# Two state rows of 64 channels in one step of a Mamba scan, with silu and softplus as single ScalarE functions

## What is computed

```python
xz = u @ W_in;  xr, z = split(xz)              # 192 channels each
x = silu(causal_conv4(xr) + conv_b)
dt, Bm, Cm = split(x @ W_x)                    # 6, 16, 16 columns
delta = softplus(dt @ W_dt + b_dt)
A = -exp(A_log)                                # 192 x 16
h_t = exp(delta_t * A) * h_(t-1) + (delta_t * x_t) * B_t     # per channel and state n
y_t = sum over n of h_t * C_t
out = ((y + x * D) * silu(z)) @ W_out
```

## Time and profile before

| | |
|---|---|
| median of 3 runs | 2221.36 us (2218.45 to 2224.84) |
| the profiled execution | 2221.17 us, span 2219.4 us |
| busy, share of the span | PE 82%, DVE 88%, ACT 51%, POOL 88% |
| granted TensorE clock, mean | 0.94 |
| DMA | 398 MB, mean 179 GB/s |

### The profile page before, as it was taken

The page is one execution under the profiler, slowest core; times in us unless marked ns, Lnnn a source line. Parts: engine busy times, 40 slices in busy tenths (PEclk is TensorE's granted clock), DMA queues, the critical chain, the costliest instruction groups (busy, mean ns, idle before and its releaser), DMA issues. The chain is left out here.

```text
span 2219.4 us, 16413 instructions
## 1 busy us (share of the span) xinstructions
PE 1823.8 (82%) x4490; PEld 698.3 (31%) x4490; DVE 1958.8 (88%) x1276; ACT 1136.3 (51%) x1316; POOL 1957.2 (88%) x856
## 2 busy tenths in 40 slices
PE   5597889798798799789879779879878888876777
PEld 2232233233233333233333223323323333222322
DVE  2898898778998998998999898999889899899995
ACT  3657464645745644644655544644575564453331
POOL 0897988797998997998999899799899989899995
PEclk9798899899999899999999999999999999999898
DMA  3465556436556656664655665565655665566673
GB/s 83 170 206 147 173 176 176 139 130 222 157 189 213 175 170 204 175 197 172 206 156 197 217 176 199 190 162 190 207 155 173 202 191 185 192 205 184 219 218 81
DMA packets 119592, 398.24 MB, mean 179 GB/s; under 512 B 17788, under 2 KB 22156, under 8 KB 119500
## 3 DMA queue, kind: packets, MB, share of 16 engines
q1 hardware_dynamic: 119500, 397.20, 57.7%
HBM read 386.70 MB, written 6.29 MB: 177 GB/s over the span
## 5 line engine op out<-in xcount | busy, mean ns | idle before, releaser
L898 POOL TENSOR_TENSOR ring<-ring,c_ring 128x1024 f32<-128x1024 f32 x576 | 1348.4, 2367 | 113.7 <-DVE ring L835 110.6
L495 PE MATMUL y_ps<-ring,wp 128*128 128x512 f32 x2304 | 1183.8, 627 | 53.0 <-DVE yv_rows L815 28.2
L835 DVE TENSOR_TENSOR_SCAN ring<-a_ring,b_ps 128x1024 f32<-128x1024 f32 x424 | 968.2, 2284 | 28.5 <-ACT a_ring L616 0.3
L495 PEld LDWEIGHTS y_ps<-ring,wp 128*128 128x128 f32 x2304 | 449.9, 199 | 525.0 <-issue 409.6
L801 DVE TENSOR_TENSOR b_ps<-u_ab,b_ps 128x1024 f32<-128x1024 f32 x256 | 310.2, 1212 | 95.6 <-PE b_ps L487 69.2
L616 ACT ACTIVATE a_ring<-delta_ab,neg_a 128x1024 f32<-128x1024 f32 x256 | 290.6, 1142 | 199.2 <-DVE ring L835 194.0
L835 DVE TENSOR_TENSOR_SCAN ring<-b_ps,b_ring 128x1024 f32<-128x1024 f32 x152 | 344.6, 2273 | 27.7 <-ACT b_ps L616 12.3
L892 POOL TENSOR_TENSOR b_ring<-u_ab,b_ring 128x1024 f32<-128x1024 f32 x128 | 306.6, 2396 | 59.2 <-DMA b_ring<-b_rows 59.1
L616 ACT ACTIVATE a_ring<-delta_m,neg_a 128x1024 f32<-128x1024 f32 x168 | 192.3, 1145 | 238.8 <-DVE ring L835 238.7
L487 PE MATMUL b_ps<-b_in,sel 96*128 96x512 bf16 x512 | 164.2, 404 | 102.1 <-DVE ring L835 101.4
L801 DVE TENSOR_TENSOR b_ps<-u_m,b_ps 128x1024 f32<-128x1024 f32 x168 | 203.0, 1209 | 19.6 <-PE b_ps L487 19.6
(11 more groups left out here) (91 smaller groups left out, 1262.0 us busy)
## 6 DMA issues: line engine op xcount, KB each, us to landing
c_ring<-c_rows SPq DMA_DIRECT2D x384, 512.0 KB, 4.8
c_ring<-c_rows SPq DMA_DIRECT2D x384, 256.0 KB, 4.1
b_ring<-b_rows SPq DMA_DIRECT2D x128, 512.0 KB, 4.8
b_ring<-b_rows SPq DMA_DIRECT2D x48, 256.0 KB, 5.2
out<-io SPq DMA_DIRECT2D x16, 192.0 KB, 2.4
io<-x SPq DMA_DIRECT2D x6, 384.0 KB, 4.9
b_in<-parts SPq DMA_DIRECT2D x36, 64.0 KB, 2.0
dt_in<-parts SPq DMA_DIRECT2D x72, 24.0 KB
```

Source lines behind the costliest of these rows:

```text
L495: nc.tensor.matmul(half(y_ps[:, :], j), ident, half(ring[:, g % RING, :], j), start=(n == 0), stop=(n == NS - 1)).then_inc(g_summed, 1)
L835: nc.vector.tensor_tensor_scan(out=h, data0=a, data1=b, initial=0.0, op0=ALU.mult, op1=ALU.add).then_inc(h_ready, 1)
L898: nc.gpsimd.tensor_tensor(r, r, c_ring[:, g % C_RING, :], ALU.mult).then_inc(g_ready, 1)
```

## The change

A step now treats 64 channels and two states: partitions 0 to 63 hold the channels with state 2m, partitions 64 to 127 the same channels with state 2m+1. Two steps g and g+1 (sub 0 and 1) cover the tile's 128 channels for the two states. So an item still has 48 steps. What follows from it:

- delta and u are made once a tile (`delta_in`, `u_in`) and copied by eight DMAs of 64 x 1024 into doubled forms (`delta`, `u_two`); all users of them wait for these (`wait_two`).
- The two steps of a pair share a row pair of C in tiles 0 and 1: `c_ring` has three slots for four, and a slot serves two steps there and one in tile 2. Each load of C or B is two DMAs to 64 partitions.
- The sum uses a matrix of two stacked identities of 64 (`stack`). A job sums one column half of two steps: sub 0 into partitions 0 to 63 of `y_ps`, sub 1 into 64 to 127. SUM_LAG is 3.
- Silu and softplus are one ScalarE function each, without halved weights. Silus, gates and dts are put in twos; table loads stand between them and the exps.
- `x_out` and `parts3` hold one half instead of two, and "bc_in" comes twice.
- BY_POOL has 156 steps, and the slot tables of PREP, POST and the first items are new.

```diff
-BY_POOL = {ROWS: (2, 8, 13, 17, 19, 23, 26, 30, 31, 37, 47),
...
+BY_POOL = {ROWS: (5, 8, 14, 18, 20, 23, 25, 28, 31, 37, 41, 43, 47), FWD: (5, 10, 13, 15, 19, 20, 23, 25, 35, 41, 42),
+           BWD: (0, 6, 8, 13, 15, 19, 21, 23, 25, 31, 33, 39, 40, 45, 47)}
...
-PE_ORDER = ("ahead", "sum_0", "jobs", "sum_1")
+PE_ORDER = ("ahead", "sum", "jobs")
...
+PREP = dict(xr=(0, 2, 4.5, 6.5, 8.5, 10.5), silu=(4, 4, 8.5, 8.5, 12.5, 12.5), skip=(14, 16, 16), dbl=(14.5, 19),
+            dt=(25, 25, 34, 34, 52.2, 52.2), u=(26, 35, 54), two=(32, 48, 64), z=(20, 22, 24, 24, 27, 27))
...
+                elif name == "two":
+
+                    q = phase_of(kind, pair, i)
+                    wait(sp, h_ready, NS * (q - 1))
+                    sp.wait_ge(K["set_ready"][kind], 3 * pair + nth(i))
+                    for src, dst in ((delta_in, delta), (u_in, u_two)):
+                        for sub in range(2):
+                            for e in range(2):
+                                sp.dma_start(dst[e * DM:(e + 1) * DM, q % 2, sub, :],
+                                             src[sub * DM:(sub + 1) * DM, :]).then_inc(two_loaded[q % 2], 16)
...
+            def sum_half(pair_of, j):
+
+                n = 2 * pair_of % NS
+                pe.wait_ge(g_ready, 2 * pair_of + 2)
                 if n == 0:
-                    wait(pe, y_taken, 2 * (g // NS - 1) + j + 1)
-                nc.tensor.matmul(half(y_ps[:, :], j), ident, half(ring[:, g % RING, :], j),
-                                 start=(n == 0), stop=(n == NS - 1)).then_inc(g_summed, 1)
...
+                for sub in range(2):
+                    last = nc.tensor.matmul(half(y_ps[sub * DM:(sub + 1) * DM, :], j), stack,
+                                            half(ring[:, (2 * pair_of + sub) % RING, :], j),
+                                            start=(n == 0), stop=(n == NS - 2))
+                last.then_inc(g_summed, 1)
...
-                    nc.scalar.activation(half(xs[:, k, :], j), src, ACT.Identity, bias=bias)
-                    nc.scalar.activation(src, src, ACT.Tanh, bias=bias).then_inc(th_ready, 1)
...
+                    table("silu_and_others")
+                    empty(u, nc.scalar.activation(half(xs[:, k, :], j), src, ACT.Silu, bias=sm[:, m_of(k), 4:5]))
...
+                    table("softplus")
+                    empty(unit, nc.scalar.activation(half(delta_in[:, :], j), src, ACT.Softplus, bias=sm[:, m_of(k), 5:6]))
...
-                wait(dve, g_summed, 2 * (g - RING + 1))
+                wait(dve, g_summed, 2 * ((g - RING) // 2 + 1))
```

More of the change, by code:

```diff
@@ L33 @@
 RING = 6
-C_RING = 4
+C_RING = 3
 C_LEAD = 3
@@ L87, in fills_prep @@
         out.append((at["xr"][u] + 1, "xr", u))
-        out.append((at["xr"][u] + 2, "silu", u))
+        out.append((at["silu"][u], "silu", u))
     for k in range(TILES):
@@ L97, in fills_prep @@
     for k in range(TILES):
-        out.append((at["exp"][k], "dt_exp", k))
-        out.append((at["ln"][k], "dt_ln", k))
         out.append((at["u"][k], "u", k))
+        out.append((at["two"][k], "two", k))
     if kind != BWD:
@@ L197, in plan @@
         parts.append(item(FWD, p - 1, *fills))
-        parts.append(item(BWD, p - 1, fills_prep(ROWS, p + 1) if p + 1 < PAIRS else fills_prep(FWD, p)))
-    parts.append(item(FWD, PAIRS - 1, fills_post(BWD, PAIRS - 2), fills_prep(BWD, PAIRS - 1)))
-    parts.append(item(BWD, PAIRS - 1))
+        prep = fills_prep(ROWS, p + 1) if p + 1 < PAIRS else fills_prep(FWD, p)
+        parts.append(item(BWD, p - 1, late, own(prep)))
+        late = spill(prep)
+    prep = fills_prep(BWD, PAIRS - 1)
+    parts.append(item(FWD, PAIRS - 1, late, fills_post(BWD, PAIRS - 2), own(prep)))
+    parts.append(item(BWD, PAIRS - 1, spill(prep)))
     parts.append(alone(fills_post(BWD, PAIRS - 1)))
-    step = unit = use = 0
+    step = unit = 0
     for part in parts:
@@ L209, in plan @@
                 takes = name in BANKED
-                tanh = name in ("xr", "z")
-                slot[n] = (name, kind, pair, i, unit if takes else None, use if tanh else None)
+                slot[n] = (name, kind, pair, i, unit if takes else None)
                 unit += takes
-                use += tanh
     return parts
@@ new lines, in job @@
+                    sp.wait_ge(K["c_cut"][kind], 2 * pair + i + 1)
+                    wait(sp, g_ready, STEPS * (n - 1))
+                    sp.dma_start(half(b_rows[slot].rearrange("b n t -> (b n) t"), i), x_out[0:B_ROWS, :]).then_inc(c_kept, 16)
+                    sp.dma_start(half(c_rows[slot].rearrange("b n t -> (b n) t"), i), x_out[C_AT:X_ROWS, :]).then_inc(c_kept, 16)
+                    if n:
+                        landed(sp, "dt", ITEMS[n - 1]["kind"], ITEMS[n - 1]["pair"], 4, 5)
@@ new lines, in job @@
+                    landed(sp, "dbl", kind, pair, i)
+                    for g in range(3):
+                        sp.dma_start(half(b_in[B_ROWS * g:B_ROWS * (g + 1), slot, :], i),
+                                     parts3[0:B_ROWS, g, :]).then_inc(K["bc_loaded"][kind], 16)
+                    for q, (g, _) in enumerate(DT_TERMS):
+                        sp.dma_start(half(dt_in[2 * RANK * q:2 * RANK * (q + 1), :], i),
+                                     parts3[B_ROWS:SPLIT_ROWS, g, :]).then_inc(K["dt_loaded"][kind], 16)
+                elif name == "two":
[7 more added lines that the diff above has]
+                                             src[sub * DM:(sub + 1) * DM, :]).then_inc(two_loaded[q % 2], 16)
```

423 lines of the change are left out of this document (187 added, 236 removed).

## The result

The changed kernel took 2302.16 us (median of 4 runs, 2297.41 to 2314.84), the kernel before 2222.16 us beside it: a ratio of 1.037, 95% interval 1.0326 to 1.0414. The change made it slower by 80 us. The forecast was 2126 us, with 0.11 for slower.

The account below looks back on a forecast made before the run. VectorE and GpSimd, 88% busy each and joined by a ring of six buffers, were taken to bound the kernel together, with waits between. Terms -81 -15 -45 +10 +21 +9 -7 +13 = -95 from 2221.2 gave 2126 us; range 2065 to 2190.

Parts of the forecast that it names:

- Engines' work, -81: VectorE loses 87 us of work and GpSimd 75 net; both engines need it, so the mean, -81 us, was counted.
- the tanh waits (-15): VectorE's waits for ScalarE's tanh, 21 us, are removed; some will be found again before the scan: -15 us (0 to -21).
- ScalarE's batches, +21: Batch at slot 4, with its table loads, delays B's spread 1.9 us on 11 items: +21 us (0 to +50); other batches nothing.
- Sums, -45: Sums by 64 columns run side by side on TensorE, halving VectorE's 88.8 us wait for B's spread: -45 us (0 to -89).
- TensorE gives nothing: Rival, chance 0.17: TensorE's sum halves don't overlap or its clock falls, so the -45 goes: 2150 to 2190 us, say 2171.
- The copies, +13: Copies are hidden by 16 steps, except at slot 32, where eight issues delay C's row 2.1 us on 11 items: +13 us.
- The start, +9: Before scan 0, copy, exp load and dbl's shared buffer add time, dropped functions save 5.9 us: +9 us (+4 to +14).
- The gap before the image item, -7: VectorE's 14.15 us wait before the first FWD item shrinks, as u and its copy come earlier: -7 us (-14 to +5).
- More waits in TensorE's row, +10: Sums need an odd step's product, so GpSimd bursts block TensorE a step earlier, B's spread behind: +10 us (0 to +30).
- C's rows starve GpSimd: Rival, chance 0.04: each of 35 copies behind the first costs its 4.8 us of issue, +155 us, giving 2281 us.
- the rival on ScalarE's batches: Rival, chance 0.07: about 91 returns to exp each cost load and decay, 2.4 us, +197 us, giving 2323 us.
- All three signs of being wrong: Forecast is wrong if VectorE waits for decays above 50 us, `c_ring` waits pass 60, or granted clock falls below 0.85.

Follow-up runs that it names:

- run 10: Kernel before, own slots and 152 steps, silu and softplus as one function a half, stand-ins from exp's table, so nearly no table loads: 2167.01 us.
- run 9: Kernel before with single functions in the change's batches, slots and 156 steps, stand-ins from exp's table, so nearly no table loads: 2202.96 us.
- run 6: Kernel before with real silu and softplus as one function each, in the change's batches, slots and 156 steps; no halves, no copies: 2229.92 us.
- run 3: Changed kernel, each paired sum's weight padded with zeros to 128 columns, so its two instructions can't run side by side: 2342.22 us.
- run 2: Changed kernel, the eight copies still issued but each moving 16 of 1024 columns: 2207.56 us.
- run 4: Kernel before, rows of B and C for tiles 0 and 1 loaded as two transfers to 64 partitions each, same bytes: 2243.68 us.
- run 1: Changed kernel with tanh and abs from exp's table in place of silu and softplus, so nearly no table loads: 2275.95 us.
- run 18: Kernel before with real single functions in its own slots, halves of gates and softplus paired, and pairs of the convolution's silus too: 2165.20 us.
- run 11: Kernel before, own slots and 152 steps, real silu and softplus as one function a half, so 309 table loads: 2209.71 us.
- run 13: Changed kernel, only the copies of an item's first tile (11 of 36, none of the first item) moving 16 of 1024 columns: 2248.63 us.
- run 14: Changed kernel, only the copies of an item's second and third tiles (22 of 36) moving 16 of 1024 columns: 2259.77 us.

## Why the prediction was wrong

The way to 2302 is walked by the runs, from the 2226 measured beside run 10: functions' work -59 (run 10: 2167), the change's slots and its 156 steps +36 (run 9: 2203), loads +27 (run 6: 2230), the doubled form with sums at their old price +112 (run 3: 2342), sums by halves -40 (2302). Of the +112, the copies' bytes are 95 as run 2 has them, and half rows 20 as run 4 has them in the kernel before; the forecast had 13 for the copies and nothing for half rows. That is the largest miss; the work of engines (37 us) and the slots and loads (42 us) come behind it. The forecast's terms, one by one:

- **Engines' work, -81.** Busy times fell by 68 and 67, not 87 and 75 (VectorE's groups add up to 2023 us before and 1942 after, 81 less, but that counts overlaps of neighbours twice: its busy time was 1959 and 1891), and all of the work with the tanh waits (-15) was worth 59 in run 10, not 96: TensorE, at full sums, did the same work in less time, and the wait for B's spread rose from 88.8 to 119.3. This step took two leading engines' gain whole, though a third stood at 82%. That it is the third engine which holds them is argued from that wait; run 3 adds that TensorE's sums are worth 40 us.
- **ScalarE's batches, +21.** The one at slot 4 was priced, the others were called free. Run 1 gives 26 for loads; the batches' and slots' own part is 36 (in the form before; where in the slots it lies is open, and run 18 speaks against the pairs of the convolution). Loads take 1.28 us, and in the trace after, too, the next function follows at once (66.39 + 1.28 us, next at 67.69). 287 loads more between runs 10 and 11 cost 43 us of the end, 0.15 us each. The Trainium skill, ScalarE: Activation LUTs, What ACT_TABLE_LOAD costs, has 1.38 us of drain on top; of it nothing is visible here. By row, then, not by page. Silu and softplus took what the tanh row said, within 5%:

```profile
66.39 1.28 ACT L628 ACT_TABLE_LOAD   x1 [14.67 <-PE bank L529]
67.69 1.27 ACT L709 ACTIVATE delta_in<-bank,wp 128x512 f32<-128x512 f32 x2
...
L672 ACT ACTIVATE xs<-bank,wp 128x512 f32<-128x512 f32 x72 | 46.1, 684 | 13.6 <-PE bank L553 13.1
L709 ACT ACTIVATE delta_in<-bank,wp 128x512 f32<-128x512 f32 x72 | 45.6, 684 | 0.4
```

- **Sums, -45.** Right in kind and nearly in size: 40 (run 3). Four instructions take 1.08 us, as the earlier trace rows promised:

```profile
1064.44 1.08 PE L508 MATMUL y_ps<-ring,wp 128*64 128x512 f32 x4
```

  The rival "TensorE gives nothing" was half true in its reason: the clock fell to 0.778, the mean of one sum instruction was 786 ns, and TensorE was busy 1649 us and not 1400. Its effect did not follow: at clock 0.913 and full sums the kernel is slower. The Trainium skill, TensorE: Matmul & The Clock Gate, HAM oscillation, says that waits between bursts of matmuls bring the half clock; the traces agree in sign (busy 82% at a mean clock of 0.94 before, 72% at 0.778 after).
- **The copies, +13: the step that failed.** "The traffic does not rise" and "hidden by 16 steps" asked whether the doubled forms are there when their tile begins. They nearly always were. What was late stood beside them: the rows of C and B behind them in the same queue, and the next tile's softplus, which waits until the copies have read `delta_in`. The copies' bytes cost 95 us (run 2): 53.5 with the first tiles, most at the place that I named, and 42.4 at places where I counted nothing (runs 13, 14). The step also counted megabytes at 310 GB/s, the mean over transfers to 128 and to 64 partitions. Transfers to 64 ran at 245 and copies within the core at 200, so fewer bytes kept the queue busy longer; that alone does not make rows so late (run 4). Half rows were given no price, and cost 20 us there. The four doubled parts of u took a median of 1.08 us an issue, not 0.6. How the 95 us divide between late rows and the late softplus, and what the burst, the rate and a C ring of three rows have in the former, is open.
- **The start, +9:** 21.5. 6 of it are the copies' bytes (first scan at 79.48 in run 2). The rest I read from the timelines: it is mostly the second half of dbl, kept back by the shared buffer until the first half's transfers had landed, so that its last part stood behind the constants on VectorE, and nine issues of b_in and dt_in behind that. VectorE's last part, and TensorE's first product of dt:

```profile
57.29 0.68 DVE L862 TENSOR_TENSOR parts<-bank,parts 44x512 bf16<-44x512 f32 x1
...
65.73 1.01 PE L529 MATMUL bank<-dt_in,w_dt_parts 72*128 72x512 bf16 x2 [23.47 <-DMA dt_in<-parts]
```

- **The gap before the image item, -7:** 0; it ends on the copy (13.80 us) as it ended on u.
- **More waits in TensorE's row, +10.** VectorE waits 30.1 us for sums, which it hardly did before; I can't part it from late products.

The rival "C's rows starve GpSimd", with a chance of 0.04, had the right wait. Its reason was only in part right: it blamed the time to issue a copy, 4.8 us on all 35, while run 2 still issues all of them and is 95 us faster. What costs is mainly the bytes; B's rows come late beside C's, and softplus waits for the copies. That a first tile's copy costs 4.9 us, close to its 4.8, is luck; one elsewhere costs 1.9. Its 2281 us is no nearer to 2302 than the 2323 of the rival on ScalarE's batches, of whose +197 run 1 shows 26. All three signs of being wrong that the prediction named came true: waits for decays of 54.6 us (42.8 and 11.8), `c_ring` waits of 126.5, a clock of 0.778.

## What to carry to other kernels

Before forecasting that transfers stay hidden, ask what stands behind them in the same queue with how many steps of slack, and who must wait to write the buffer that they read, and not only whether they arrive in time themselves. Read the queue's rate for each shape of transfer: here those to half the partitions, and copies within the core, were dearer per byte. What two leading engines give up need not be worth its whole size where a third is nearly as full (59 us of 96 here). A product that stands in TensorE's row before its data have landed can show up as a wait of some other engine for TensorE; look in TensorE's own waits for a transfer and try the product a slot later.

## What the hardware showed that I had not expected

The same 397 MB took 57.7% of the queue with two thirds of them in transfers to 128 partitions, and 72.6% with nearly all in transfers to 64. Yet the kernel of the second kind was only 20 us slower, while 74 MB of copies, with rows behind them in the queue and a softplus waiting for them, cost 95 us. Loads with a slowest dimension of 2 ran the queue at 18.5% and the kernel at 6001 us. TensorE at a mean granted clock of 0.778 gave a faster kernel (2302) than at 0.913 with more columns to write (2342). 287 table loads of 1.28 us each cost the end 0.15 us each.
